# Second attention: the masking of the scores above the threshold moves from VectorE to GpSimd

## The reference, cut to what matters

```
draft = einsum('bhqd,bhkd->bhqk', qr, kr) + causal          # causal: most negative float above the diagonal
_, draft_indices = top_k(draft, num_remain)                  # num_remain = 128
mask = full(neg); mask[draft_indices] = 0; mask = where(causal_future, neg, mask)
attn = softmax(draft / sqrt(32) + mask);  out = attn @ v
```

## Time and profile before

| engine | busy us | share of the span | instructions |
|---|---|---|---|
| PE | 4809.9 | 78% | 23480 |
| DVE | 3892.3 | 63% | 11322 |
| ACT | 3356.3 | 54% | 7666 |
| POOL | 263.0 | 4% | 149 |

### The profile page before, as it was taken

The page is one execution under the profiler, slowest core; times in us unless marked ns, Lnnn a source line. Parts: engine busy times, 40 slices in busy tenths (PEclk is TensorE's granted clock), DMA queues, the critical chain, the costliest instruction groups (busy, mean ns, idle before and its releaser), DMA issues. The chain is left out here.

```text
span 6177.2 us, 81244 instructions
## 1 busy us (share of the span) xinstructions
PE 4809.9 (78%) x23480; PEld 3476.0 (56%) x23480; DVE 3892.3 (63%) x11322; ACT 3356.3 (54%) x7666; POOL 263.0 (4%) x149
## 2 busy tenths in 40 slices
PE   7997999999999989944667667767666666766787
PEld 2446888888744444423546546645645655656444
DVE  2654555555522335638888888888888888885222
ACT  1213555454400002148888888888888888884001
POOL 1330000000000003300000000000000000000000
PEclk9998999999999999975555555555555555555888
DMA  2223111112121122320110000110010010000211
GB/s 113 70 65 78 46 44 44 44 44 47 44 95 44 48 81 64 71 49 8 22 22 22 18 22 5 22 22 22 18 22 12 15 22 22 22 1 5 86 61 54
DMA packets 275861, 249.37 MB, mean 40 GB/s; under 512 B 170240, under 2 KB 210320, under 8 KB 275472
## 3 DMA queue, kind: packets, MB, share of 16 engines
q1 hardware_dynamic: 274928, 245.08, 15.0%
q0 software_dynamic: 544, 0.07, 0.0%
HBM read 167.51 MB, written 77.59 MB: 40 GB/s over the span
## 5 line engine op out<-in xcount | busy, mean ns | idle before, releaser
L894 ACT ACTIVATE a_sign<-a_x,a_state 128x256 bf16<-128x256 f32 (+6 forms) x2240 | 1832.4, 819 | 311.1 <-DVE a_state L1015 196.9
L839 PE MATMUL a_ps_o<-a_v,a_probT 128*128 128x32 f32 x4608 | 1018.0, 389 | 343.6 <-ACT a_probT L870 342.6
L839 PEld LDWEIGHTS a_ps_o<-a_v,a_probT 128*128 128x128 f32 x4608 | 1037.4, 333 | 368.0 <-ACT a_probT L870 367.5
L820 PE MATMUL a_ps_s<-a_k,a_q 128*128 128x512 bf16 (+3 forms) x1536 | 493.2, 464 | 592.7 <-DVE a_x L1122 552.3
L831 PE MATMUL a_ps_t<-a_ident,a_prob 128*128 128x128 f32 x2304 | 601.8, 425 | 151.0 <-DVE a_prob L1112 147.4
L629 ACT ACTIVATE a_prob<-a_ps_s,a_shift 128x128 f32<-128x128 f32 (+7 forms) x512 | 379.7, 742 | 561.6 <-DVE a_shift L657 447.6
L321 PE MATMUL p_ps_qkv<-p_w,p_hT 128*128 128x512 f32 x1536 | 675.5, 597 | 3.3 <-ACT p_hT L359 2.3
L820 PEld LDWEIGHTS a_ps_s<-a_k,a_q 128*128 128x128 bf16 x1536 | 162.7, 129 | 831.0 <-DVE a_x L1122 660.5
L831 PEld LDWEIGHTS a_ps_t<-a_ident,a_prob 128*128 128x128 f32 x2304 | 509.7, 254 | 161.0 <-issue 138.3
L607 PE MATMUL a_ps_o<-a_v,a_probT 128*128 128x32 f32 x4608 | 594.0, 276 | 0.0
L607 PEld LDWEIGHTS a_ps_o<-a_v,a_probT 128*128 128x128 f32 x4608 | 566.4, 195 | 27.1 <-issue 4.5
(11 more groups left out here) (177 smaller groups left out, 5582.0 us busy)
## 6 DMA issues: line engine op xcount, KB each, us to landing
a_q<-qk SPq DMA_DIRECT2D x256, 256.0 KB, 4.7
qk<-p_qkT SPq DMA_DIRECT2D x32, 960.0 KB, 6.2
p_h<-h SPq DMA_DIRECT2D x32, 512.0 KB, 7.0
a_k<-qk SPq DMA_DIRECT2D x256, 64.0 KB, 5.0
o<-a_o SPq DMA_DIRECT2D x32, 512.0 KB, 3.3
m_o<-o SPq DMA_DIRECT2D x32, 512.0 KB, 5.3
m_h<-h SPq DMA_DIRECT2D x32, 512.0 KB, 4.9
p_w<-in_wqkv SPq DMA_DIRECT2D x16, 768.0 KB, 11.5
```

Of the source, the lines that this page charges most:

```text
L820: nc.tensor.matmul(ps_s[:, n % 2, a:a + w], q[:, y, head, i * P:(i + 1) * P], k[:, y, a:a + w], start=(y == 0), stop=False, skip_group_che ...
L839: mm = nc.tensor.matmul(ps_o[:, n, :], probT[:, n % 2, b * P:(b + 1) * P], v[:, b * DH:(b + 1) * DH], start=(b == 0), stop=(b == i))
L894: ins = nc.scalar.activation(sign[:, off(i):off(i) + w], x[:, par, at:at + w], ACT.Sign, scale=-1.0, bias=state[:, par, 0, n:n + 1], accum ...
```

## The change

GpSimd gets a program in `kept_attention`. For each ranked tile, in the order of DVE's counts (`RANK_ORDER`), it compares the scores with the threshold and multiplies by -1e30 (one operation, fp32), drains, and adds the scores (a second operation, in place in `below`). DVE's L1028 is gone; its count stays, and its result `above` is no longer read. DVE's eight largest of tile c now wait for GpSimd's mask of that tile (`below_ready`), and they stand two tiles behind the count, across the borders of the parts. GpSimd starts a pair when its last threshold is there (`last_ready`), and it writes the mask of tile c when DVE has read that of tile c-2 (`nine_ready`), since `below` has two buffers. The core of the diff:

```
-                    def rank_steps(n, r): ...      # count, mask (scalar_tensor_tensor), eight largest
+        RANK_ORDER = [*range(0, TT - 2), TT - 1, TT - 2, *range(TT + 1, NS), TT]
+            @block.gpsimd
...
+                    def mask_above(c):
+                        n = RANK_ORDER[c]
+                        m, i = RANKED[n]
+                        at, w = ps_seg(m, i), (i + 1) * P
+                        out = below[:, c % 2, 0:w]
+                        if c == 0:
+                            wait_alone(pool, last_ready, s, const_in, 64)
+                        if not (isinstance(s, int) and s == 1 and c < 2):
+                            wait_alone(pool, nine_ready, (s - 1) * NS + (c - 1), const_in, 64)
+                        nc.gpsimd.tensor_scalar(out, x[:, y, at:at + w], state[:, y, 0, n:n + 1], MASKED, ALU.is_ge, ALU.mult)
+                        pool.drain()
+                        nc.gpsimd.tensor_tensor(out, out, x[:, y, at:at + w], ALU.add).then_inc(below_ready, 1)
...
                         if p < PASSES - 1:
                             ins.then_inc(t_ready, 1)
+                        else:
+                            ins.then_inc(last_ready, 1)
...
+                    def count_above(c):
+                        n = RANK_ORDER[c]
+                        m, i = RANKED[n]
+                        at, w = ps_seg(m, i), (i + 1) * P
+                        nc.vector.tensor_scalar(above[:, c % 2, 0:w], x[:, y, at:at + w], state[:, y, 0, n:n + 1], None,
+                                                ALU.is_ge, ALU.add, accum_out=exact[:, n:n + 1])
+                    def nine_below(c):
+                        n = RANK_ORDER[c]
+                        w = (RANKED[n][1] + 1) * P
+                        wait_alone(dve, below_ready, (s - 1) * NS + (c + 1), const_in, 64)
+                        nc.vector.max(nine[:, n, 1:9], below[:, c % 2, 0:w]).then_inc(nine_ready, 1)
+                    def rank_some(first, last):
+                        for c in range(first, last):
+                            count_above(c)
+                            if c >= 2:
+                                nine_below(c - 2)
                             dve.drain()
...
-                    RANKS = [[*range(0, TT - 2), TT - 1], [TT - 2, *range(TT + 1, NS)], [TT], (), ()]
+                    RANKS = [(0, TT - 1), (TT - 1, NS - 1), (NS - 1, NS), (0, 0), (0, 0)]
...
+                            rank_some(*RANKS[p])
                             if p == 2:
+                                nine_below(NS - 2)
+                                nine_below(NS - 1)
+                                dve.drain()
                                 choose()
```

More of the change, by code:

```diff
@@ L745, in kept_attention @@
         exp_done, prob_ready = sem("exp_done"), sem("prob_ready")
+        last_ready, below_ready, nine_ready = sem("last_ready"), sem("below_ready"), sem("nine_ready")
         turn_done, probT_ready, pv_done, o_ready = sem("turn_done"), sem("probT_ready"), sem("pv_done"), sem("o_ready")
@@ L927, in _, with slot @@
                 over_slots(act, slot)
+            @block.gpsimd
+            def _(pool):
+                def slot(s, par, st):
+                    y = 1 - par
+                    def mask_above(c):
[10 more added lines that the diff above has]
+                        nc.gpsimd.tensor_tensor(out, out, x[:, y, at:at + w], ALU.add).then_inc(below_ready, 1)
+                    if st["keep"]:
+                        for c in range(NS):
+                            mask_above(c)
+                over_slots(pool, slot)
             @block.vector
@@ L1017, in narrow @@
                             ins.then_inc(t_ready, 1)
-                    def rank_steps(n, r):
+                        else:
+                            ins.then_inc(last_ready, 1)
+                    def count_above(c):
+                        n = RANK_ORDER[c]
                         m, i = RANKED[n]
                         at, w = ps_seg(m, i), (i + 1) * P
[L1024 to L1039, removed]
+                        nc.vector.tensor_scalar(above[:, c % 2, 0:w], x[:, y, at:at + w], state[:, y, 0, n:n + 1], None,
[10 more added lines that the diff above has]
+                                nine_below(c - 2)
                             dve.drain()
@@ L1166, in part @@
                         if st["keep"]:
-                            rank_some(RANKS[p])
+                            rank_some(*RANKS[p])
                             if p == 2:
+                                nine_below(NS - 2)
+                                nine_below(NS - 1)
+                                dve.drain()
                                 choose()
```

## The result

The changed kernel takes 6753.3 us (median of 4 runs, 6741.5 to 6758.4) beside 6181.3 for the kernel before on the same chip (4 runs, 6171.8 to 6195.4): 1.0927 times the time, 95% interval 1.0906 to 1.0949. Its profiled execution has a span of 6749.2 us, 572.0 more than before. The forecast was 6250 with a range up to 6400, so the sign was right and the size was not. All times here are medians of the fast executions; one slow execution each of the runs compare_narrow (6575.7 us) and fast_two (9810.8 us) is left out.

What follows compares the result with a forecast made beforehand. The prediction took PE to bound passes 0 and 1 and DVE passes 2 to 4. Part 2 +62, late starts -13 and blocked threshold steps +15 made +64 us: 6241 profiled, 6250 median, range 6205 to 6400.

Steps and rivals of the forecast that it cites:

- the price of GpSimd's compare: GpSimd's new first mask operation, compare and multiply: taken as 1.2 ns a column, between 0.98 and 2.04.
- masks 7 to 12: GpSimd's 4864 columns in pass 1: 17.5 us, ending 20.0 us into it, just meeting the threshold step at 19.9.
- All of DVE blocked: Rival, passes 0 and 1: GpSimd holds up counts and MAX too; +13 us a slot, +400, 6590 us; chance 0.05.
- the last wait: Part 2: DVE waits for the last mask, 384 columns, before the choosing; 0.2 us (0.1 to 0.55).
- the three signs that the prediction had named: Forecast wrong if DVE waits in passes 2-4, PE idles in passes 0-1, or counts or MAXs lengthen beside GpSimd.
- slow masks: Rival: compare at 2 ns a column or more, masks late for threshold steps; up to 8 us per slot, 6400; chance 0.28.
- Part 2: DVE's stretch from its count to the choosing grows by 2.0 us per slot, 31 x 2.0 = +62 us.
- The gain in passes 0 and 1: In 12 slots with DVE's late first count, both passes fall to the other slots' length: 12 x 1.1 = -13 us.
- Hidden growth: Rival: slack in parts 3 and 4 and ACT's outlasting DVE hide part 2's growth; +9 us, 6195; chance 0.09.
- The blocked threshold steps: Pass 1: DVE's two-input threshold operations held up beside GpSimd; 0.5 us per slot, 31 x 0.5 = +15 us.
- The estimate from the Trainium skill: GpSimd's compare at 0.86 ns a column; by it the sum would be +46 us.
- Faster: Rival: the 3.46 us of issue behind part 2's branch go away; -107 us, 6143; chance 0.04.

Runs made afterwards that it cites:

- compare_narrow: The changed kernel with GpSimd's compare on only the first 16 columns of each tile, its addition on all: 6224.1 us, 1.0076 times the kernel before.
- fast_two: The kernel before with GpSimd finishing two masks in each of parts 0 and 1 by multiply-and-add constants and addition, part 2's tile moved to part 1: 6152.3 us.
- add_narrow: The changed kernel with GpSimd's addition on only the first 16 columns of each tile, its compare on all: 6246.1 us, 1.0124 times the kernel before.
- both_narrow: The changed kernel with both GpSimd operations on only the first 16 columns of each tile, all waits kept: 6210.7 us, 1.0057 times the kernel before.
- const_form: The changed kernel with GpSimd's compare replaced by a multiply and an addition by constants, on all columns: 6237.0 us, 1.0091 times the kernel before.

## Why the prediction was wrong

**The step that failed** is the price of GpSimd's compare: "The two rows bound it, 0.98 and 2.04 ns", and "By its inputs it is nearest to the conversion; I take 1.2 ns". It is 3.34 ns a column and 0.29 us an operation. The upper bound was no bound: a two-input operation has one arithmetic step and two inputs, and says nothing of a tensor_scalar. The text did see that it could be "over both if GpSimd runs its two arithmetic steps one after the other", but that reason does not hold either (the compare alone is 2.50, the second step adds 0.84), and the case got no price.

**What hung on it.** The forecast followed masks 7 to 12 and the last one, which was enough as long as they ended before the threshold step. The whole chain of 14 masks stands only in the rival "All of DVE blocked", with "about 29 + 4 us of GpSimd" at 1.2 ns, where it fits. By the measured rates the sum is 33.9 + 21.6 + 3.4 = 58.9 us, where passes 0 and 1 have 42.1, and everything behind the choosing waits for it. One addition from the first mask to the last, against the time between the two points that hold it, shows the knee; the 0.2 us that the last wait was given does not. In part 2 of the slot shown above DVE waits 3.17 and 1.58 us for GpSimd, and PE is not busy throughout pass 1: two of the three signs that the prediction had named.

**The rival "slow masks"** had the mechanism right, and its condition, "2 ns a column or more". Its price, up to 8 us per slot, was tied to the 2.04 ns and so was the range's end at 6400. Even for 2.04 ns it was not the right sum: by its own rates the chain is then 36.6 + 4.1, some 41 us, as long as that of add_narrow (40), whose slot grew by 2.2 us. So its way of adding up late masks gave too much just below the knee, and the case above the knee had no price.

**Part 2** (+2.0 us per slot, +62) held in size: in both_narrow, where GpSimd never makes DVE wait, pass 2 is 19.44 us where it was 18.26 and pass 3 17.73 where it was 16.90 (medians of 26 slots), together +2.0. That is the +1.8 of the longer part and some 0.2 more; the wait, which made up the other 0.2 of the forecast, is not in it. The gain in passes 0 and 1 (-13) held too, 42.2 us in both kinds of slot. Their sum, +49, less some 10 us which the first ranked pair gains (its slot takes 76.9 us where it took 87.2), is close to the 35 measured. "Hidden growth" falls with it.

**The blocked threshold steps** (+0.5 us per slot) exist, but unevenly: 5.85 us instead of 2.24 in pass 1 of every second slot of the changed kernel. (The reading of the earlier trace rows passed over L80: it has two inputs, stands between the two long operations, and takes 0.16 us.) One of the long steps, on DVE, and GpSimd beside it:

```profile
4142.62 0.84 DVE L1033 TENSOR_SCALAR a_open<-a_miss 128x14 int32<-128x14 f32 x1
4143.53 0.24 DVE L1035 RECIPROCAL a_rs<-a_span 128x14 f32<-128x14 f32 x1
4143.69 1.99 DVE L1036 TENSOR_TENSOR a_new<-a_new,a_span 128x14 f32<-128x14 f32 x1
...
4146.03 0.86 DVE L1040 TENSOR_TENSOR a_new<-a_bracket,a_new 128x14 f32<-128x14 f32 x1
```

```profile
4140.16 3.28 POOL L946 TENSOR_SCALAR a_below<-a_x,a_state 128x896 f32<-128x896 f32 x1
4143.58 2.07 POOL L948 TENSOR_TENSOR a_below<-a_below,a_x 128x896 f32<-128x896 f32 x1
```

In the changed kernel it costs nothing of its own, since GpSimd is what the slot waits for at that time. In const_form it is part of what that kernel takes over both_narrow: the step of pass 0 takes 2.9 us instead of 1.9 in every second slot, and passes 0 and 1 take 42.7 there instead of 42.2. What add_narrow takes over both_narrow lies in pass 2 (20.25 us instead of 19.44; all medians).

**"All of DVE blocked"** is out: the counts of 1024 columns take 1279 ns and the MAXs 1229, as in the earlier trace rows, in a kernel where GpSimd works beside almost all of them:

```profile
L1053 DVE TENSOR_SCALAR_CACHE_REDUCE a_above<-a_x,a_state 128x1024 bf16<-128x1024 f32 x64 | 81.8, 1279 | 7.3
...
L1061 DVE MAX8 a_nine<-a_below 128x8 f32<-128x1024 f32 x64 | 78.7, 1229 | 295.7 <-POOL a_below L948 295.7
```

For these two operations this agrees with the Trainium skill, SBUF — State Buffer, section "Who interferes with whom", by which an operation of VectorE with one input in SBUF and no 2-port mode does not contend. L1033 above, with one input, was held up (0.84 us, usually 0.17); whether it ran in such a mode the runs do not show.

**The estimate from the Trainium skill**, GPSIMD Engine Reference, section "Performance versus the Vector engine" (a body of at most two arithmetic steps at 1.03 cycles per element, 0.86 ns a column), agrees with the constants form (0.82) and the copy (0.84), and not with the forms of 2.50 and 3.34. Had it been taken as a rule for the compare, it would have led further off than the forecast.

**"Faster"** did not come: the branch's issue wait in part 2 totals 107.0 us in 31 slots, as before (107.1).

## What to carry to other kernels

Before work goes to another engine, add up that engine's whole chain between the two points that hold it and compare it with the time that lies between them; below it, 29 us more of chain cost a slot 0.8 us here, and above it the slot grew by as much as the chain. Where the trace has no row of the very operation and form, neighbours of other kinds are no bounds: here forms of one instruction lay a factor of four apart, so a range over such a cost should be open upwards, or the cost measured alone first. And what waits behind a new semaphore is all that stands behind it in program order: here the choosing, and with it the next scores, PE and ACT.

## What the runs showed of the hardware

- GpSimd's tensor_scalar in fp32 showed three speeds in the forms that ran: 0.82 ns a column for multiply and add by constants, 2.50 for a single step (compare with a column, or multiply by a constant), 3.34 for compare and multiply, whether the first number is a column or a constant.
- How GpSimd's operation holds up VectorE depends on the form. A VectorE operation with two inputs ended with GpSimd's addition (the 1.99 us of L1036 above, 4143.69 to 4145.68, beside an addition from 4143.58 to 4145.65). Beside the compare and multiply such operations were held up only in its first 1.1 us or so: one of 0.86 us at 4146.03, beside a compare that began at 4145.75 and took 3.70; those later beside it took their usual 0.17 to 0.20. This came the same way in 13 slots. The one-input tensor_scalar L1033 was held up towards the compare's end, 0.84 us at 4142.62 beside one that ended at 4143.44. Why, the runs do not show.
- It works the other way too: GpSimd's constants form of 768 columns takes 1.29 us in the row of fast_two above, and 0.83 in const_form, where VectorE has no mask operation. That of 896 columns, which in fast_two comes before VectorE's first mask, takes 0.94 in both.
